# A four-stage transformer kernel: the norm, weight split, dt chain and first projections of its mamba stage interleaved; decay rows one chunk ahead; gate weights split inside the stage; attention scores at other positions

## The reference, cut to what matters

```python
x = x + mamba_and_mlp(layernorm(x))   # rmsnorm, mamba2, residual, rmsnorm, silu(gate) * up, down
x = x + lut_ffn(layernorm(x))         # 688 hidden units, weights looked up in a table of 16
x = x + attention(layernorm(x))       # 16 heads of 128, causal, 1024 tokens in each of 2 sequences
x = x + moe(layernorm(x))             # 8 experts, top 2

# mamba2, cut:
z, xb, B, C, dt = split(h @ in_proj_w)            # 512, 128, 128, 512, 8 columns
xb, B, C = silu(causal_conv4(concat(xb, B, C)))
dt = softplus(dt + dt_bias); A = -exp(A_log)
dAc = cumsum(dt * A) within a chunk of 128 tokens
Y = (C B^T * exp(dAc_q - dAc_s) * causal) @ (x * dt) + C state * exp(dAc)
state = state * exp(dAc_end) + B^T (x * dt * exp(dAc_end - dAc))
out = rmsnorm((Y + D * x) * silu(z)) @ out_proj_w

# attention, cut:
attn = softmax(causal(q @ k.T / sqrt(128))); z = attn @ v; out = z @ W_O + b_O
```

## Time and profile before

| what | value |
| --- | --- |
| median of 3 runs | 2011.61 us (2010.68 to 2011.92) |
| the profiled execution | 2013.73 us |
| its span in the trace | 2012.0 us |
| busy in the span: PE, PEld, DVE | 1760.4, 1475.8, 1357.4 us |
| busy in the span: ACT, POOL | 996.1, 648.6 us |
| mean granted clock of PE | 0.95 |
| largest part of the chain that ended last | PE 71%, DVE 15%, ACT 5%, issue 4% |

### The profile page before, as it was taken

The page is one execution under the profiler, slowest core; times in us unless marked ns, Lnnn a source line. Parts: engine busy times, 40 slices in busy tenths (PEclk is TensorE's granted clock), DMA queues, the critical chain, the costliest instruction groups (busy, mean ns, idle before and its releaser), DMA issues.

```text
span 2012.0 us, 33107 instructions
## 1 busy us (share of the span) xinstructions
PE 1760.4 (87%) x10294; PEld 1475.8 (73%) x10294; DVE 1357.4 (67%) x2831; ACT 996.1 (50%) x2011; POOL 648.6 (32%) x666
## 2 busy tenths in 40 slices
PE   3577777888999899999999799999999987999997
PEld 1344444777788788888888678888888875878876
DVE  6667555788756666666666666666666664888887
ACT  3445343555333656566555466566565651333332
POOL 6133336334333322222222232232222211343442
PEclk9888887899999999999999899999999997999998
DMA  3000010100101000000000010000000001010001
GB/s 100 1 1 1 1 43 18 48 15 7 19 1 23 22 22 21 0 21 21 21 5 15 15 30 22 0 21 21 21 21 0 5 1 47 17 32 16 16 1 42
DMA packets 59855, 37.68 MB, mean 19 GB/s; under 512 B 16537, under 2 KB 56705, under 8 KB 59777
## 3 DMA queue, kind: packets, MB, share of 16 engines
q1 hardware_dynamic: 59776, 36.71, 6.5%
HBM read 34.60 MB, written 2.10 MB: 18 GB/s over the span
## 4 chain that ended last, share of the span: by engine, by line
PE 71%; DVE 15%; ACT 5%; issue 4%; DVEq 3%; POOL 1%; ACTq 0%; DMA 0%; POOLq 0%
PE psum L52 13%; PE psum L53 12%; PE psum L54 12%; PE psum L1611 6%; PE psum L1624 3%; PE psum L1601 3%; PE psum L1603 3%; PE psum L1602 3%; PE psum L1625 3%; PE psum L1632 3%; DVE table_leaves L579 2%; DVE mamba_conv_sum L1117 2%; DVE mamba_mixed L1139 1%; ACT attn_probs L1677 1%; DVE attn_pt_lo L1719 1%
## 5 line engine op out<-in xcount | busy, mean ns | idle before, releaser
L1763 POOL TENSOR_SCALAR attn_probs<-attn_probs,attn_inverse 128x128 f32<-128x128 f32 (+7 forms) x256 | 192.4, 752 | 578.6 <-DVE attn_inverse L1727 577.8
L1672 ACT ACTIVATE attn_pt_hi<-psum 128x512 fp32r<-128x512 f32 (+3 forms) x384 | 184.2, 485 | 216.9 <-PE psum L1611 214.9
L1719 DVE TENSOR_TENSOR attn_pt_lo<-psum,attn_pt_hi 128x512 fp32r<-128x512 f32 (+3 forms) x384 | 210.4, 552 | 67.7 <-ACT attn_pt_hi L1672 65.5
L1677 ACT ACTIVATE attn_probs<-attn_probs,attn_neg_max 128x128 f32<-128x128 f32 (+7 forms) x256 | 197.9, 773 | 99.8 <-DVE attn_neg_max L1723 99.5
L1611 PE MATMUL psum<-ident,attn_probs 128*128 128x128 f32 x1152 | 190.4, 277 | 33.9 <-DVE attn_pt_lo L1719 18.8
L1723 DVE CUSTOM_DVE_ANT_0 attn_probs<-psum,attn_mask 128x128 f32<-128x128 f32 (+7 forms) x256 | 192.5, 753 | 17.7 <-PE psum L1603 10.0
L1624 PE MATMUL psum<-attn_pt_hi,attn_v_hi 128*128 128x512 f32 (+3 forms) x384 | 161.9, 422 | 26.2 <-DVE attn_pt_lo L1719 19.4
L1611 PEld LDWEIGHTS psum<-ident,attn_probs 128*128 128x128 f32 x1152 | 137.9, 142 | 55.8 <-DVE attn_pt_lo L1719 24.9
L2039 POOL TENSOR_TENSOR moe_hid_lo<-moe_hidden,moe_hid_hi 128x512 fp32r<-128x512 f32 x64 | 83.0, 1297 | 196.4 <-ACT moe_hid_hi L2012 196.4
L1601 PE MATMUL psum<-attn_k_hi,attn_q_hi 128*128 128x512 f32 (+3 forms) x384 | 133.8, 349 | 2.6 <-DVE attn_neg_max L1723 2.5
L1625 PE MATMUL psum<-attn_pt_lo,attn_v_hi 128*128 128x512 f32 (+3 forms) x384 | 134.3, 350 | 0.0
(11 more groups left out here) (329 smaller groups left out, 5239.3 us busy)
## 6 DMA issues: line engine op xcount, KB each, us to landing
attn_qkv_raw<-in_L_attn_W_Q_dram SPq DMA_DIRECT2D x32, 128.0 KB, 2.2
attn_qkv_raw<-in_L_attn_W_K_dram SPq DMA_DIRECT2D x32, 128.0 KB, 2.4
attn_qkv_raw<-in_L_attn_W_V_dram SPq DMA_DIRECT2D x32, 128.0 KB, 2.5
attn_wo_raw<-in_L_attn_W_O_dram SPq DMA_DIRECT2D x16, 256.0 KB, 2.9
moe_gu_raw<-_L_ffn_gate_up_proj_dram SPq DMA_DIRECT2D x8, 512.0 KB, 3.8
x_in<-_attn_hidden_states_dram SPq DMA_DIRECT2D x4, 512.0 KB, 5.5
x_tok<-_attn_hidden_states_dram SPq DMA_DIRECT2D x4, 512.0 KB, 6.1
moe_down_raw<-in_L_ffn_down_proj_dram SPq DMA_DIRECT2D x8, 256.0 KB, 4.0
```

The lines of the kernel that those rows point to most:

```text
L1677: act.activation(probs_view(e), probs_view(e), ACT.Exp, bias=stat(neg_max, e), scale=-1.0, accum_out=stat(sums, e)).then_inc(exp_done, 1)
L1719: dve.tensor_tensor(lo, work_view(e), hi.bitcast(F32), ALU.subtract).then_inc(work_done, 1)
```

## The change

Four edits, none of which adds or removes arithmetic:

1. The start of the mamba stage becomes one list of steps. `first_steps` now holds the norm's four groups (`norm_in`: stats, apply, split), the ten first projection blocks and the six parts of the dt chain. SP loads two groups of x, then `in_raw`, then the other two; the fifteen small loads are issued by ACT. ACT splits the weights' high parts before any norm group, POOL their low parts between the roots of the second and third group. `out_hi` is made at the seventh block.
2. Within a chunk the rows and `row_exp` of chunk c+1 are made at the end of B(c-1), C(c-2) (a new step `rows`), and A(c) becomes: transposes, mask, scores on PE; `xb_tok`, `decay` on ACT.
3. POOL splits the gate weights in four quarters of 128x512 after chunks 2, 4, 5 and 6 of the first sequence.
4. `score_at` changes, so that the eight score tiles stand at positions 0, 1, 2, 3, 5, 6, 8, 9.

```diff
-    first_steps = [("project", 0, m) for m in range(IP)]
+    first_norm = [[("norm_in", i, "stats"), ("norm_in", i, "apply"), ("norm_in", i, "split")] for i in range(GROUPS)]
+    first_project = [("project", 0, m) for m in range(IP)]
+    first_dt = [("dt", 0, n) for n in range(6)]
+    (n0, n1, n2, n3), p, dt = first_norm, first_project, first_dt
+    first_steps = [n0[0], n1[0], n0[1], n2[0], n0[2], n1[1], n3[0], n1[2], p[0], n2[1], p[1], n2[2], n3[1], p[2], n3[2],
+                   dt[0], p[3], dt[1], p[4], dt[2], p[5], dt[3], p[6], dt[4], p[7], dt[5], p[8], p[9]]
...
-            parts = [[("A", c, None)] if c < CHUNKS else [],
-                     ([("B", c - 1, None)] if 1 <= c <= CHUNKS else []) + ([("C", c - 2, None)] if c >= 2 else []),
+            parts = [([("rows", 0, None)] if c == 0 else []) + ([("A", c, None)] if c < CHUNKS else []),
+                     ([("B", c - 1, None)] if 1 <= c <= CHUNKS else []) + ([("C", c - 2, None)] if c >= 2 else [])
+                     + ([("rows", c + 1, None)] if c + 1 < CHUNKS else []),
...
+            if kind == "norm_in" and m == "apply":
+                norm_in["turn"](pe, c)
...
+            elif kind == "rows":
                 pe.wait_ge(done["steps"], CHUNKS // QUADS * b + c // QUADS + 1)
                 pe.wait_ge(done["leaves"], n)
+                if c:
+                    pe.wait_ge(done["state_done"], n)
...
+    GATE_AT = {2: 0, 4: 1, 5: 2, 6: 3}
...
-        gate, gate_raw = ff["gate"], ff["gate_raw"]
-        pool.tensor_copy(gate[0][:, :, :], gate_raw[:, :, :])
+        def feed_gate(m):
+            k, half = divmod(m, 2)
+            cols = slice(half * FF // 2, (half + 1) * FF // 2)
...
+                if c in GATE_AT:
+                    feed_gate(GATE_AT[c])
...
-            score_at = {0: 0, 2: 1, 3: 2, 5: 3, 6: 4, 8: 5, 9: 6, 11: 7}
+            score_at = {0: 0, 1: 1, 2: 2, 3: 3, 5: 4, 6: 5, 8: 6, 9: 7}
...
-            norm_groups(norm_mamba, range(HALF))["scalar"](act)
+            with nc.allow_non_contiguous_dma(reason="small vectors, one element for each partition"):
+                for dst, src in small:
+                    act.dma_start(dst, src).then_inc(small_loaded, 16)
             in_split["scalar"](act)
-            norm_groups(norm_mamba, range(HALF, GROUPS))["scalar"](act)
...
-            norm_groups(norm_mamba, range(GROUPS))["gpsimd"](pool)
+            norm_groups(norm_mamba, range(HALF))["gpsimd"](pool)
             in_split["gpsimd"](pool)
+            norm_groups(norm_mamba, range(HALF, GROUPS))["gpsimd"](pool)
```

More of the change, by code:

```diff
@@ L949, in step @@
             elif kind == "A":
+                if c == 0:
+                    pe.wait_ge(done["sums_copied"], 1)
+                    pe.wait_ge(done["masks"], 4)
                 pe.wait_ge(done["state_done"], n)
@@ L1024, in scalar @@
     def scalar(act):
-        prep_scalar(act)
+        act.wait_ge(dma["small"][0], dma["small"][1])
+        act.activation(w["A_log"][:, :], w["A_log"][:, :], ACT.Exp).then_inc(done["decay_rate"], 1)
         def step(b, e, bank, old):
@@ L1030, in step @@
             tile = b * CHUNKS + (c or 0)
-            if kind == "project":
+            if kind == "norm_in" and m == "split":
+                norm_in["high"](act, c)
+            elif kind == "dt":
+                dt_scalar(act, m)
+            elif kind == "project":
                 what, at = place_of(e)
                 count = PER[what] * b + at
+                if c == 0 and m == 0 and old is None:
+                    act.wait_ge(done["conv_scaled"], 1)
+                if c == 0 and m == XBC_BLOCKS:
+                    act.wait_ge(done["prep"], 1)
+                    act.activation(w["out"][0][:, :, :], w["out_raw"][:, :, :], ACT.Copy).then_inc(dma["out_scaled"], 1)
                 act.wait_ge(done["projected"], (PER["conv"] + PER["z"]) * b + IP * c + m + 1)
@@ L1055, in step @@
                                ACT.Copy).then_inc(done["xb_copied"], 1)
+                act.wait_ge(done["masked"], n + 1)
+                for h in range(HEADS):
+                    last = act.activation(decay[:, c % 2, h, :], s.psum[:, h // REP, h % REP * P:(h % REP + 1) * P],
+                                          ACT.Exp, bias=minus_cum[:, tile, h:h + 1])
+                last.then_inc(done["leaves"], 1)
+            elif kind == "rows":
                 act.wait_ge(done["rows_ready"], 1 + n + 1)
@@ L1061, in step @@
                 last.then_inc(done["row_exp"], 1)
-                act.wait_ge(done["masked"], n + 1)
-                for h in range(HEADS):
-                    last = act.activation(decay[:, c % 2, h, :], s.psum[:, h // REP, h % REP * P:(h % REP + 1) * P],
-                                          ACT.Exp, bias=minus_cum[:, tile, h:h + 1])
-                last.then_inc(done["leaves"], 1)
             elif kind == "B":
@@ L2379, in _ @@
             pe.wait_ge(s.consts_ready, CONSTS)
-            norm_groups(norm_mamba, range(GROUPS))["tensor"](pe)
             mamba["tensor"](pe)
```

250 lines of the change are left out of this document (136 added, 114 removed).

## The result

The changed kernel took 1995.67 us (median of 4 runs, 1995.19 to 1996.11), the kernel before 2011.72 us beside it; the ratio is 0.9921, with a 95% interval of 0.9904 to 0.9938. It is 16 us faster, where 35.5 us were forecast. The profiled execution took 1995.56 us, its span is 1993.8 us, 18.2 less than the span before (that execution was 2.1 us over its median).

What follows compares the result with a forecast made beforehand. Start and chunk loop were taken as bound by chains between engines, the attention as held by one recurring PE wait. +1.5 (start) - 17 (loop) - 20 (attention) = -35.5, so 2011.6 becomes 1976 us; range 1958 to 1996.

Steps and rivals of the forecast that it cites:

- The attention: Attention bodies and last sections: PE's wait for score tile 7 before the transposes goes; -20 us, bounds -22 and 0.
- The term for ACT's extra exponential: Attention, positions 1 to 3: one more exponential ahead of the output's copy costs 0.1 us per half with scores, 2 us.
- The rows: Chunk loop: rows and their exponential made a chunk early take 2.0 us per chunk off the way to the outputs.
- Mostly covered: Chunk loop: the new wait for `state_done` is mostly hidden, as DVE's state follows PE's outputs by 1 us during C (2 us).
- The loop: Chunk loop in all: -17 us, with 1 us of contention from the gate quarters included; bounds 29 gained, 27 lost.
- The gate quarters: Chunk loop: POOL's four quarters of the gate split cost DVE contention, 0 to 3.3 us, taken as 1.
- The start: Start up to the first chunk's `mixed`: 1.3 us later by the new order, taken as +1.5; bounds -13 (rival) and +5.
- The walk: Start: the new order followed with the old durations, operation by operation, putting `mixed` at 95.8 us against 94.48 before.
- A: Start: idle links overlap better than reckoned, -13 instead of +1.5, total 1962 us; chance 0.18.
- B: Attention keeps its time because ACT is late for the output's copy; total 1996 us; chance 0.12.
- C: Chunk loop gains nothing because DVE's own work is the period; total 1993 us; chance 0.13.
- D: Chunk loop slower: rows and `row_exp` delay the next block, 1.92 us per chunk, +27; total 2020 us; chance 0.04.

Runs made afterwards that it cites:

- loop_only: Kernel before with only the rows and row_exp made one chunk ahead (step `rows`): 1998.07 us, ratio 0.9937.
- gate_only2: Kernel before with only the gate weights' split moved into the chunk loop as four quarters: 2009.94 us, ratio 0.9993.
- loop_att_gate2: Changed kernel but with the old start (rows ahead, new `score_at`, gate quarters in the loop): 1977.03 us, ratio 0.9831.
- loop_att: Kernel before with the rows one chunk ahead and the new `score_at`, without new start or gate quarters in the loop: 1986.70 us, ratio 0.9858.
- att_only: Kernel before with the new `score_at` alone: 2002.49 us, ratio 0.9950.
- wait_act: Changed kernel with the wait for DVE's state ahead of the rows taken by ACT, ahead of row_exp, not by PE: 1988.94 us, ratio 0.9896.
- gate_start: Changed kernel with POOL's four gate quarters behind the norm, ahead of `out_lo`, and none in the loop: 1987.74 us, ratio 0.9871.
- start_only: Changed kernel with the rows back in A and the old `score_at`, leaving new start and gate quarters: 2024.69 us, ratio 1.0059.

## Why the prediction missed half

**The attention (-20; -14.2 from the first `attn_qkv_lo` to the end).** The mechanism held: the wait for tile 7 was POOL's, and it went. A body gained 1.10 where 1.34 less 0.2 was forecast. From the first `attn_qkv_lo` to the router the old `score_at` takes 1001.3, 1001.6 and 1001.2 us (before, loop_only, gate_only2), the new one 983.2 in the changed kernel and 983.3 in loop_att_gate2: 18 of the 20 are there. Three things failed. The term for ACT's extra exponential was 2 us, but 0.1 for each of the 28 halves in the bodies is 2.8. In the last section 1.6 of wait were to go, but PE's next wait, for `attn_z_raw`, grew from 0.7 to 1.8 there, so 0.5 is left. And I gave the clock no part. Where some later bodies begin at the lower clock, the same stretch is 988.6 (loop_att) and 990.8 (att_only), so the edit gives 12.7 and 10.5 there. In the changed kernel no later body does, but its MoE is 3.9 longer than before, the first stretch at 0.70 instead of 0.77. That is not this edit's: from the router to the end loop_only, with the old `score_at`, takes 347.4, and loop_att_gate2, with the new one, 344.6. All profiles lie at 344.6 to 344.9 or at 347.4 to 348.9, with the same instructions; why is open.

**The rows (-18 without the quarters).** Nearly right: -16.6 and -17.1 alone. "Mostly covered" for the new wait was right in the net, though moving it gave another 6 us (wait_act).

**The loop (-17; -7.9).** By the loops of loop_att (219.9), loop_att_gate2 (225.1) and the changed kernel (229.4), the miss of 9.1 has three parts: 0.6 in the rows, 4.2 in the quarters and 4.3 behind the new start (both below).

**The gate quarters (+1).** This is the step that failed most plainly. I took 1 out of 0 to 3.3; two pairs of kernels (loop_att and loop_att_gate2, gate_start and the changed kernel) show 5.2 and 5.5. The ratio 2.38 to 1.14 that I scaled from is of apply operations with one tensor input; the taps have two, and three of them took 4.11 instead of 2.40 beside a subtraction of 1.82. The Trainium skill (SBUF — State Buffer, Who interferes with whom) says that a DVE instruction with two inputs in SBUF contends with a GpSimd instruction that reads it. The traces agree: the tap is such an instruction, and the longest took 2.23 us beside the subtraction instead of 0.75. The forecast named the rule and put 5 us on it, but kept 1 in the sum; measured are 4.2 to 4.5 more than the 1. The taps' own busy time bears it out: 5.0 more in the first pair (47.2 to 52.2), 6.1 in the second (46.7 to 52.8). The price depends on the loop: 2.4 in the old one.

**The start (+1.5; +4.7).** It is a sum of two misses. Taking the split out is worth 5.9 (gate_only2), not 4.3. The interleaving itself costs 10.6 (88.6 to 99.2), not 5.8. The walk was right to 0.9 us up to convolution 2. Then the last dt matmuls and block 3 took from 58.80 to 63.3, at half clock up to 62.45, in place of 3.0 us, and dt*A started 1.2 us later than in the walk. `out_lo`, which the walk had overlooked, landed beside dt*A (0.69 to 2.67), so that dt*A ended at 84.3 and not at 81.5. The rest held: the first z block behind the sums took 2.9 us where the walk had 2.7, and from the end of dt*A to `mixed` it is 14.9 instead of 14.3.

**What the start does to the loop (not forecast).** With the same rows and quarters, the loop is 225.1 behind the old start and 229.4 behind the new; without quarters 219.9 and 223.9; with the old rows and quarters 239.7 and 243.1 (gate_only2, start_only). That is 4.3, 4.0 and 3.4 us, each no more than equal loops can differ by, but three times the same way. The forecast had this at nothing, without a reason. The loops by stretches, old start and then the changed kernel:

```profile
88.60:313.70 225.10, 181.80 (x970) 112.42 (x970) 150.13 (x315) 110.76 (x265) 109.29 (x112) 0.86 0.03 10
```

```profile
99.20:328.60 229.40, 186.91 (x970) 115.43 (x970) 151.74 (x315) 110.95 (x265) 108.92 (x112) 0.83 0.03 10
```

As many matmuls, 5.1 us more of busy PE, at a lower clock. That the clock is the cause fits, but no run set the clock alone; why it is lower behind the new start stays open. The new start does not fix it: wait_act, with the same start, has its loop at 0.87.

**The rivals.** None of A to D came true as named: the start did not overlap, the attention did not keep its time, the loop did not gain nothing, and row_exp did not make it slower. That the measured 1995.67 is B's 1996 is luck: B has -17 in the loop and nothing in the attention, and measured are -7.9 and -14.2. The sum of the misses is 3.2 in the start, 9.1 in the loop and 5.8 from the attention on, less 0.8 between: the 17.3 us between 35.5 and 18.2.
